# Four batches per step in two buffers, in place of two batches in four, in the last loop of a graph-attention and slot-expert kernel

## The chip, the cores and the metric

The kernel runs on one core of a Trainium2 chip. The metric is the device time of one execution in microseconds; the median of three runs of the kernel before is 3202.54 us (3198.05 to 3209.62).

## The reference

Input `x` is 64 batches of 128 tokens with 384 features. The reference adds a graph-attention layer to it, and then a mixture-of-slots layer with 8 x 4 experts:

```
x = x + L0_gnn_ref(layernorm(x), adj, ...)      # attention with bias adj, then a feed-forward layer
x = x + L0_ffn_ref(layernorm(x), ...)           # slots, 32 experts, then:
#   out2 = einsum('bGkpd,bGksp->bGksd', o, comb2)      expert rows back to slots
#   out  = einsum('bGPd,bGgP->bGgd', out2, comb1)      slots back to tokens
```

The last two products are merged in the kernel: the dispatch stage has already multiplied the two combine matrices into one 128 x 128 matrix per batch, `combT`. What is left for the last stage is, for each of the 64 batches, one product of that matrix with the 128 x 384 rows of expert output, plus the 128 x 384 rows of the residual.

## The kernel before, in words

There are four stages, each in its own block, one after the other: the attention layer, `dispatch`, `experts` and `combine`. Only `combine` (from L1707) is touched.

`combine` walks over the 64 batches in 8 rounds of `ROUND` = 8 batches. A round is cut into steps of `G` batches, one per buffer, so that there are `BUF = ROUND // G` buffers; with `G` = 2 there are four buffers of two batches. Each buffer is three tiles: `o_sb[i]` ("c_o", expert rows), `ct[i]` ("c_ct", combine matrices) and `y[i]` ("c_y", the result), and `G` PSUM banks. Whatever `G` is, there are 8 batches' worth of each.

- SP's queue: `body` waits until the matmuls that read the buffer a round ago are done (`full`, L1743), then issues one load of expert rows (L1744) and one of combine matrices (L1745). In the first round it does not wait. After the last step of the first round it also issues one load of the residual of the last 8 batches, `late` ("c_late", L1747). The residual of the first 56 batches (`early`) is in the chip's memory already, in the tile "slots2T".
- TensorE: waits for both loads (`landed[i]`), then does one matmul per batch (L1758), each into its own bank. A float32 matmul of 128 x 128 by 128 x 384 shows in the trace as two matmul instructions, so x4 stands for two batches and x8 for four. A bank must have been read by VectorE a round ago (`added`, L1757).
- VectorE: waits until the store that used `y[i]` a round ago has landed (`stored[i]`), then adds the residual to each bank (L1773).
- ScalarE's queue: waits for the `G` additions of a step and issues one store of `y[i]` to the output (L1780). At the end it waits for all stores.

The order on each queue is that of the code; no scheduler changes it. Round 0 is written out, rounds 1 to 6 are a hardware loop (L1727), and round 7 is written out.

Of the kernel before, what the change touches and what calls it, by code (L numbers as in the profile page):

```python
# [62 lines left out]
def past(step, n):  # L63

    return not isinstance(step, int) or step >= n


def build(nc, x, adj, wq, bq, wk, bk, wv, bv, wo, bo, w1, b1, w2, b2, alpha1, gamma1, alpha2, gamma2,
# [13 lines left out]
    with ExitStack() as kernel_ctx:  # L82
# [28 lines left out]
        with ExitStack() as experts_ctx:  # L111
            slots2T = sb(experts_ctx, "slots2T", [P, E1, DC, NB, S1])

            early = slots2T[:].rearrange("p k c b j -> p (k c b j)")[:, 0:EARLY * D].rearrange("p (g d) -> p g d", d=D)
            res_landed = sem(experts_ctx, "res_landed", 16)
            with ExitStack() as ctx:
                dispatch(nc, ctx, sb, ps, sem, ident, nhalf, eps, f_w_slot2, yn_dram, comb_dram, ct_dram, slots2T)
            with ExitStack() as ctx:
                experts(nc, ctx, sb, ps, sem, ident, slots2T, f_w1, f_b1, f_w2, f_b2, o_dram, res_dram, early,
                        res_landed)  # L120
            with ExitStack() as ctx:
                combine(nc, ctx, sb, ps, sem, ct_dram, o_dram, res_dram, out, early, res_landed)
# [1584 lines left out]
def combine(nc, ctx, sb, ps, sem, ct_dram, o_dram, res_dram, out, early, res_landed):  # L1707


    G = 2  # L1710
    BUF = ROUND // G
    ROUNDS = NB // ROUND
    o_sb = [sb(ctx, f"c_o{i}", [P, G, D]) for i in range(BUF)]
    ct = [sb(ctx, f"c_ct{i}", [P, G, P]) for i in range(BUF)]
    late = sb(ctx, "c_late", [P, NB - EARLY, D])
    y = [sb(ctx, f"c_y{i}", [P, G, D]) for i in range(BUF)]
    bank = [[ps(ctx, f"c_bank{i}{g}", [P, 512]) for g in range(G)] for i in range(BUF)]
    landed = [sem(ctx, f"c_landed{i}", 32) for i in range(BUF)]
    stored = [sem(ctx, f"c_stored{i}", 16) for i in range(BUF)]
    full, added = sem(ctx, "c_full", ROUND), sem(ctx, "c_added", ROUND)  # L1720
    out_rows = out.rearrange("b n d -> (b n) d")

    def loop(eng, body):

        for i in range(BUF):
            body(0, i)
        with eng.Fori(1, EARLY // ROUND) as r:  # L1727
            for i in range(BUF):
                body(r, i)
        for r in range(EARLY // ROUND, ROUNDS):  # L1730
            for i in range(BUF):
                body(r, i)

    def rows_of(t, r, i):

        return t[bass.ds(r * (ROUND * P) + i * G * P, G * P), :].rearrange("(g p) d -> p g d", p=P)

    with nc.Block() as block:
        @block.sync
        def _(sp):  # L1740
            def body(r, i):
                if past(r, 1):
                    sp.wait_ge(full.sem, full.at(r - 1, G * (i + 1)))  # L1743
                sp.dma_start(o_sb[i][:], rows_of(o_dram, r, i)).then_inc(landed[i].sem, 16)  # L1744
                sp.dma_start(ct[i][:], ct_dram[bass.ds(r * ROUND + i * G, G)].rearrange("g p n -> p g n")).then_inc(landed[i].sem, 16)  # L1745
                if isinstance(r, int) and r == 0 and i == BUF - 1:
                    sp.dma_start(late[:], res_dram[EARLY * P:NB * P, :].rearrange("(g p) d -> p g d", p=P)  # L1747
                                 ).then_inc(res_landed.sem, 16)
            loop(sp, body)

        @block.tensor
        def _(pe):
            def body(r, i):
                pe.wait_ge(landed[i].sem, landed[i].at(r, 32))
                for g in range(G):
                    if past(r, 1):
                        pe.wait_ge(added.sem, added.at(r - 1, G * i + g + 1))  # L1757
                    pe.matmul(bank[i][g][:, 0:D], ct[i][:, g, :], o_sb[i][:, g, :], start=True, stop=True).then_inc(full.sem, 1)  # L1758
            loop(pe, body)

        @block.vector
        def _(dve):
            def body(r, i):
                if past(r, 1):
                    dve.wait_ge(stored[i].sem, stored[i].at(r - 1, 16))
                for g in range(G):
                    if isinstance(r, int) and r * ROUND >= EARLY:
                        dve.wait_ge(res_landed.sem, 16 * (EARLY // ROUND + 1))
                        x_of = late[:, r * ROUND + i * G + g - EARLY, :]
                    else:  # L1770
                        x_of = early[:, bass.ds(r * ROUND + i * G + g, 1), :].rearrange("p o d -> p (o d)")
                    dve.wait_ge(full.sem, full.at(r, G * i + g + 1))  # L1772
                    nc.vector.tensor_tensor(y[i][:, g, :], bank[i][g][:, 0:D], x_of, ALU.add).then_inc(added.sem, 1)  # L1773
            loop(dve, body)

        @block.scalar
        def _(act):
            def body(r, i):
                act.wait_ge(added.sem, added.at(r, G * (i + 1)))
                act.dma_start(rows_of(out_rows, r, i), y[i][:]).then_inc(stored[i].sem, 16)  # L1780
            loop(act, body)
            for s in stored:
                act.wait_ge(s.sem, 16 * ROUNDS)
# [24 lines left out]
```

## Time and profile before

| | us |
|---|---|
| median of three runs | 3202.54 |
| the three runs | 3209.62, 3198.05, 3202.54 |
| profiled execution, its own time | 3206.89 |
| span of the profiled execution | 3205.1 |
| last matmul of `experts` ends | about 3113.7 of the span |
| first load of `combine` issued | 3118.07 of the span |

The profiled execution's own time is 1.8 us over its span. The last stage is the stretch from 3118 us to the end of the span, 87 us. Times below are microseconds from the start of the span. The DMA share of a stretch is the mean busy share of the 16 DMA engines; since packets overlap within an engine it reads a little over 1 when they are full. The granted clock of TensorE is 1.00 at 2.4 GHz and 0.50 at 1.2 GHz.

### The profile page before, as it was taken

What the parts mean: (1) busy time and instruction counts of PE and PEld (TensorE: products, weight loads), DVE (VectorE), ACT (ScalarE), POOL (GpSimd) and SP (SyncE); (2) the same over time, 40 slices, a digit from 0 to 9 for tenths busy, and PEclk for the clock granted to TensorE, in tenths of its full rate; (3) what the DMA queues carried; (4) which work ended last, traced back from release to release, by engine and by line L of the source; (5) the groups of instructions that cost most, each with busy time, mean ns of one, the idle gap of its engine ahead of it and who ended that gap; (6) DMA issues with size and microseconds to landing.
All of it is one profiled execution on the core that took longest, in us unless ns stands there. A gap on an engine that the chain in (4) does not pass through costs nothing. (4 is left out here: it accounts for less than half of the span.)

```text
span 3205.1 us, 63021 instructions
## 1 busy us (share of the span) xinstructions
PE 2945.6 (92%) x21523; PEld 2821.3 (88%) x21523; DVE 1867.8 (58%) x2989; ACT 1541.1 (48%) x3982; POOL 1474.4 (46%) x1486
## 2 busy tenths in 40 slices
PE   3999999999999999999999858888799999999986
PEld 3899999999999999999999847777799999999982
DVE  4456556565655656565655525545476777777754
ACT  3354554545454554545454435455445554545430
POOL 0334444343434444343444434343276777676750
PEclk9999999999999999999999979899899999999999
DMA  4000101010100101010110123433466666666869
GB/s 125 29 24 29 39 25 44 25 44 23 42 27 25 44 25 44 25 44 23 35 34 25 34 82 107 123 104 93 147 212 203 213 199 209 205 217 206 264 224 365
DMA packets 289909, 320.75 MB, mean 100 GB/s; under 512 B 23688, under 2 KB 289416, under 8 KB 289800
## 3 DMA queue, kind: packets, MB, share of 16 engines
q1 hardware_dynamic: 281128, 307.17, 30.6%
q10 hardware_dynamic: 8704, 12.58, 1.1%
q8 instruction: 45, 0.74, 0.1%
q14 instruction: 32, 0.26, 0.0%
HBM read 260.97 MB, written 58.72 MB: 100 GB/s over the span
## 5 line engine op out<-in xcount | busy, mean ns | idle before, releaser
L1537 PE MATMUL u_bank<-x_in,x_w 128*128 128x256 f32 x4608 | 574.1, 283 | 5.6 <-DVE x_w L1625 5.6
L1537 PEld LDWEIGHTS u_bank<-x_in,x_w 128*128 128x128 f32 x4608 | 569.2, 192 | 5.8 <-issue 5.8
L927 POOL TENSOR_TENSOR hT_lo<-h_tmp,hT_hi 128x512 fp32r<-128x512 f32 x192 | 247.9, 1291 | 473.3 <-DVE hT_hi L815 473.3
L1694 POOL TENSOR_TENSOR x_aT<-x_act,x_aT 128x512 fp32r<-128x512 f32 x128 | 299.5, 2340 | 181.9 <-ACT x_aT L1602 181.9
L388 PE MATMUL m_bank<-yT_hi,w_hi 128*128 128x256 f32 x1152 | 339.6, 295 | 0.0
L388 PE MATMUL m_bank<-yT_lo,w_hi 128*128 128x256 f32 x1152 | 324.5, 282 | 0.0
L388 PE MATMUL m_bank<-yT_hi,w_lo 128*128 128x256 f32 x1152 | 323.7, 281 | 0.0
L1690 POOL TENSOR_TENSOR x_w<-raw,x_w 128x768 fp32r<-128x768 f32 x128 | 274.2, 2142 | 105.1 <-DVE x_w L1633 105.1
L661 ACT ACTIVATE h_tmp<-m_bank,b1c 128x256 f32<-128x256 f32 x384 | 160.8, 470 | 329.8 <-PE m_bank L388 329.4
L1593 ACT ACTIVATE x_gelu<-u_bank,x_b1T 128x256 f32<-128x256 f32 x256 | 121.9, 476 | 409.6 <-PE u_bank L1537 409.6
L1549 PE MATMUL o_bank<-x_w,x_aT 128*128 128x384 f32 x1536 | 287.8, 335 | 1.8 <-POOL x_aT L1694 1.8
L1625 DVE TENSOR_TENSOR x_w<-raw,x_w 128x1536 fp32r<-128x1536 f32 x128 | 225.6, 1763 | 99.5 <-ACT x_w L1576 99.5
L388 PE MATMUL f_bank<-w_hi,hT_hi 128*128 128x384 f32 x768 | 279.7, 364 | 1.0 <-POOL hT_lo L927 1.0
L1549 PEld LDWEIGHTS o_bank<-x_w,x_aT 128*128 128x128 f32 x1536 | 262.1, 188 | 2.2 <-issue 2.2
L388 PE MATMUL f_bank<-w_lo,hT_hi 128*128 128x384 f32 x768 | 259.9, 338 | 0.0
L388 PE MATMUL f_bank<-w_hi,hT_lo 128*128 128x384 f32 x768 | 259.6, 338 | 0.0
L628 ACT ACTIVATE s_sb<-s_sb,nmax 128x128 f32<-128x128 f32 x512 | 198.0, 389 | 63.2 <-DVE nmax L775 63.2
L815 DVE CAST hT_hi<-h_tmp 128x512 fp32r<-128x512 f32 x192 | 81.7, 426 | 240.9 <-ACT h_tmp L661 240.9
L388 PEld LDWEIGHTS m_bank<-yT_lo,w_hi 128*128 128x128 f32 x1152 | 217.5, 189 | 4.1
L388 PEld LDWEIGHTS m_bank<-yT_hi,w_hi 128*128 128x128 f32 x1152 | 216.2, 188 | 4.1
L388 PEld LDWEIGHTS m_bank<-yT_hi,w_lo 128*128 128x128 f32 x1152 | 217.3, 189 | 0.0
L1651 DVE SCALAR_TENSOR_TENSOR x_act<-u_bank,x_b1T,x_gelu 128x256 f32<-128x256 f32 x256 | 119.8, 478 | 138.3 <-ACT x_gelu L1593 138.3
(213 smaller groups left out, 7303.8 us busy)
## 6 DMA issues: line engine op xcount, KB each, us to landing
raw<-in_L_ffn_w_dram SPq DMA_DIRECT2D x384, 384.0 KB, 4.8
ws_raw<-in_L_ffn_w_slot_dram SPq DMA_DIRECT2D x32, 576.0 KB, 4.2
x_in<-in_x_dram SPq DMA_DIRECT2D x32, 384.0 KB, 3.4
x_res<-in_x_dram SPq DMA_DIRECT2D x32, 384.0 KB, 4.1
residual<-f_sb SPq DMA_DIRECT2D x32, 384.0 KB, 2.5
yn<-yn_sb SPq DMA_DIRECT2D x32, 384.0 KB, 2.5
d_yn<-yn SPq DMA_DIRECT2D x64, 192.0 KB
expert_out<-x_o SPq DMA_DIRECT2D x64, 192.0 KB, 3.1
```

The source lines that it names most:

```text
L388: mm = pe.matmul(dst, left, right, start=start and c == 0 and j == 0, stop=stop and c == n - 1 and j == 2)
L628: nc.scalar.activation(s, s, ACT.Exp, bias=nmax[:, t, h:h + 1], accum_out=ssum[:, t, h:h + 1]).then_inc(p_ok.sem, 1)
L661: nc.scalar.activation(h_tmp[i % 2][:, half, :], m_bank[i % 2][:, half, :], ACT.Silu, bias=b1c[:, 2 * i + half:2 * i + half + 1]).then_inc ...
L815: nc.vector.tensor_copy(hT[i % 3][0][:], h_tmp[i % 2][:]).then_inc(hh.sem, 1)
L927: nc.gpsimd.tensor_tensor(hT[i % 3][1][:], h_tmp[i % 2][:], hT[i % 3][0][:].bitcast(F32), ALU.subtract).then_inc(hl.sem, 1)
L1537: mm = pe.matmul(u_bank[n % BANKS][:, g, :], w1s[i % 2][a][:, c, g, c2 * P:(c2 + 1) * P], xT[e % 2][b][:, c, :], start=c == 0 and j == 0, ...
L1549: mm = pe.matmul(o_bank[e % 2][t][:, 0:D], aTs[i % 2][a][:, c2, t * P:(t + 1) * P], w2s[i % 2][b][:, c2, :], start=i == 0 and c2 == 0 and ...
L1593: nc.scalar.activation(gel[:, c2, :], u_bank[n % BANKS][:, 1, :], ACT.Gelu_apprx_tanh, bias=b1T[:, HID // P + n, bass.ds(x, 1)]).then_inc( ...
L1625: nc.vector.tensor_tensor(w1s[i % 2][1][:], raw1[i][:], w1s[i % 2][0][:].bitcast(F32), ALU.subtract).then_inc(w1_lo.sem, 1)
L1651: nc.vector.scalar_tensor_tensor(out=aT[i % 2][:, c2, :], in0=u_bank[n % BANKS][:, 0, :], scalar=b1T[:, n, bass.ds(x, 1)], in1=gel[:, c2, ...
L1690: nc.gpsimd.tensor_tensor(w2s[i % 2][1][:], raw2[i][:], w2s[i % 2][0][:].bitcast(F32), ALU.subtract).then_inc(w2_lo.sem, 1)
L1694: nc.gpsimd.tensor_tensor(aTs[i % 2][1][:], aT[i % 2][:], aTs[i % 2][0][:].bitcast(F32), ALU.subtract).then_inc(al.sem, 1)
```

## The change

`G` goes from 2 to 4, and with it `BUF` from 4 to 2. Every tile keeps its total size: two buffers of four batches in place of four of two. Each load and each store is twice as large, and there are half as many. The contiguous piece that a packet moves stays as it was (one row of 384 or of 128 floats). A buffer is refilled after four matmuls in place of two, and a store is issued after four additions in place of two.

```
 def combine(nc, ctx, sb, ps, sem, ct_dram, o_dram, res_dram, out, early, res_landed):
 
 
-    G = 2
+    G = 4
     BUF = ROUND // G
     ROUNDS = NB // ROUND
     o_sb = [sb(ctx, f"c_o{i}", [P, G, D]) for i in range(BUF)]
```

The instructions of TensorE, VectorE and GpSimd keep their kinds and their order. On SP's queue the start of the last stage reads so before, where a tile's number is that of its buffer:

```order
L1744 DMA c_o0<-expert_out 128x2x384
L1745 DMA c_ct0<-combT 128x2x128
L1744 DMA c_o1<-expert_out 128x2x384
L1745 DMA c_ct1<-combT 128x2x128
L1744 DMA c_o2<-expert_out 128x2x384
L1745 DMA c_ct2<-combT 128x2x128
L1744 DMA c_o3<-expert_out 128x2x384
L1745 DMA c_ct3<-combT 128x2x128
L1747 DMA c_late<-residual 128x8x384
```

and so in the changed kernel:

```order
L1744 DMA c_o0<-expert_out 128x4x384
L1745 DMA c_ct0<-combT 128x4x128
L1744 DMA c_o1<-expert_out 128x4x384
L1745 DMA c_ct1<-combT 128x4x128
L1747 DMA c_late<-residual 128x8x384
```

Four loads stand ahead of the residual load where there were eight. On ScalarE's queue the stores of the loop's body and of the last round change so (the register and wait instructions between them go too):

```order
-L1780 DMA out_dram<-c_y 128x2x384
+L1780 DMA out_dram<-c_y 128x4x384
 L1727 REGISTER_ALU
 L1727 COMPARE_AND_BRANCH
-L1780 DMA out_dram<-c_y 128x2x384 x4
+L1780 DMA out_dram<-c_y 128x4x384 x2
 L1738 UNCONDITIONAL_BRANCH
```

The last round has two stores in place of four, and the very last one carries four batches.

## Rows read from the trace of the kernel before

**Rows 1.** Chain of waits, window 3100 to 3206: shares of the chain by engine and line.

```profile
by line: DMA c_ct<-combT 40.6%; PE c_bank L1758 23.2%; SPq L1744 4.7%; DVE c_y L1773 3.7%; issue 3.3%; SPq L1745 3.3%; DVEq L1773 0.3%; SPq L1727 0.1%; SPq L1743 0.1%; DVEq L1772 0.1%
```

**Rows 2.** Busy time, granted clock, DMA share and GB/s by stretch.

```profile
core 0: us, PE busy (x) PEld busy (x) DVE busy (x) ACT busy (x) POOL busy (x), PEclk, DMA share, GB/s
3118.00:3205.10 87.10, 53.32 (x128) 24.69 (x128) 35.59 (x64) 0.00 (x0) 0.00 (x0) 0.90 1.01 356
3155.00:3190.00 35.00, 23.14 (x60) 10.16 (x60) 16.98 (x31) 0.00 (x0) 0.00 (x0) 1.00 1.08 388
3119.00:3130.00 11.00, 6.69 (x13) 3.81 (x14) 2.83 (x6) 0.00 (x0) 0.00 (x0) 0.58 0.98 316
...
3135.00:3138.00 3.00, 2.20 (x4) 1.17 (x4) 0.41 (x1) 0.00 (x0) 0.00 (x0) 0.53 1.07 392
3140.00:3144.00 4.00, 4.00 (x10) 2.23 (x10) 2.23 (x4) 0.00 (x0) 0.00 (x0) 0.75 0.90 275
3146.00:3150.00 4.00, 1.72 (x5) 0.85 (x6) 1.98 (x4) 0.00 (x0) 0.00 (x0) 1.00 1.06 378
3200.00:3202.00 2.00, 1.42 (x4) 0.54 (x4) 1.03 (x2) 0.00 (x0) 0.00 (x0) 1.00 0.71 258
3202.00:3203.00 1.00, 0.00 (x0) 0.00 (x0) 0.08 (x1) 0.00 (x0) 0.00 (x0) 1.00 0.00 0
```

**Rows 3.** DMA issues of the last stage: count, KB each, median us to landing.

```profile
c_o<-expert_out SPq DMA_DIRECT2D x32, 384.0 KB, 6.4
out_dram<-c_y ACTq DMA_DIRECT2D x32, 384.0 KB, 6.1
c_ct<-combT SPq DMA_DIRECT2D x32, 128.0 KB, 7.0
c_late<-residual SPq DMA_DIRECT2D x1, 1536.0 KB, 9.7
```

**Rows 4.** Tile c_ct: the second load's landing; then of all loads issued 3160 to 3190.

```profile
DMA to landing us min/median/max: 5.2/5.2/5.2
...
DMA to landing us min/median/max: 6.3/7.0/7.9
```

**Rows 5.** Tile c_y: the first store's landing (issued 3126.86), then the last store's.

```profile
DMA to landing us min/median/max: 6.8/6.8/6.8
...
DMA to landing us min/median/max: 2.5/2.5/2.5
```

**Rows 6.** Timeline, first two rounds: start, us, instruction, idle before and releaser.

```profile
3119.51 0.47 SPq L1745 DMA_DIRECT2D c_ct<-combT  x1
...
3123.01 0.47 SPq L1747 DMA_DIRECT2D c_late<-residual  x1
...
3123.31 7.90 PE L1758 MATMUL c_bank<-c_o,c_ct 128*128 128x384 f32 x16 [9.61 <-DMA c_ct<-combT]
...
3126.41 0.39 SPq L1744 DMA_DIRECT2D c_o<-expert_out  x1
...
3135.80 2.92 PE L1758 MATMUL c_bank<-c_o,c_ct 128*128 128x384 f32 x4 [4.59 <-DMA c_ct<-combT]
...
3149.83 1.55 PE L1758 MATMUL c_bank<-c_o,c_ct 128*128 128x384 f32 x4 [1.71 <-DMA c_ct<-combT]
```

**Rows 7.** Chain of waits: four batches on TensorE at the low and at full clock.

```profile
3123.31 5.33 PE c_bank L1758 x8
...
3158.17 2.97 PE c_bank L1758 x8
```

**Rows 8.** Timeline, steady part: first and last of 13 TensorE steps, a refill.

```profile
3161.92 1.55 PE L1758 MATMUL c_bank<-c_o,c_ct 128*128 128x384 f32 x4 [0.80 <-DVE c_y L1773]
...
3163.65 0.37 SPq L1744 DMA_DIRECT2D c_o<-expert_out  x1
...
3190.16 1.55 PE L1758 MATMUL c_bank<-c_o,c_ct 128*128 128x384 f32 x4 [0.81 <-DVE c_y L1773]
```

**Rows 9.** Timeline, the last step.

```profile
3199.86 0.94 PEld L1758 LDWEIGHTS c_bank<-c_o,c_ct 128*128 128x128 f32 x4 [1.52 <-DMA c_ct<-combT]
...
3200.91 1.17 DVE L1773 TENSOR_TENSOR c_y<-c_bank,c_late 128x384 f32<-128x384 f32 x2 [1.29 <-PE c_bank L1758]
...
3202.12 0.38 ACTq L1780 DMA_DIRECT2D out_dram<-c_y  x1
```

More of the change, by code:

```diff
@@ L1707, in combine @@
 def combine(nc, ctx, sb, ps, sem, ct_dram, o_dram, res_dram, out, early, res_landed):
-    G = 2
+    G = 4
     BUF = ROUND // G
```

## Prediction

> **What bounds the kernel now.** Only the last stage changes, so I read that stage alone: first the chain of waits from 3100 on, then busy time by stretch, then the DMA issues with their time to landing, then the timeline of the first rounds, a steady piece and the end. What the reader is to see: the chain spends 40.6% of its time in loads of combine matrices and 23.2% in matmuls [rows 1], which looks like a stage bound by the round trip of its buffers. The stretches say otherwise. From 3155 to 3190 the DMA engines have a share of 1.08 and move 388 GB/s [rows 2]; TensorE is busy 23 of these 35 us and VectorE 17, so neither is the limit. One step of two batches moves 0.393 MB of expert rows, 0.131 MB of matrices and 0.393 MB of output [rows 3], 0.917 MB, which is 2.36 us at 388 GB/s; the steps themselves start at 3161.92 and, 12 steps later, at 3190.16 [rows 8], which is 2.35 us each. So the steady part runs at the rate of the DMA engines, and the chain only shows which transfer happened to be waited for.
>
> The whole stage moves 32 x 0.917 MB and the residual's 1.57 MB, 30.9 MB, or 79.7 us at 388 GB/s, and lasts 87.1 us [rows 2]. The 7.4 us between are: 1.0 us before the first byte (3118 to 3119); the first 11 us at 316 GB/s, which cost 11 x (1 - 316/388) = 2.0 us; a slump at 3140 to 3144, 4 x (1 - 275/388) = 1.2 us; and the end: 2 us at 258 GB/s (0.7 us), 1.0 us with no byte moved, and about 1.1 us of the last 2.1 us [rows 2]. That sums to 7.0 us. The bytes, the packets (same rows, same sizes) and the matmuls don't change. So the question is only what becomes of these 7 us, and whether two buffers still keep the DMA engines full.
>
> **The steady part with two buffers.** What the trace shows of a transfer with nothing ahead of it is the last store: issued at 3202.12, no byte moved before 3203.0, landed after 2.5 us [rows 2, 5, 9]. Its 0.393 MB take 1.0 us at 388 GB/s, so a transfer costs 1.5 us beside its bytes, 0.9 ahead of them and 0.6 behind. A new load of four batches is 1.05 MB, 2.7 us; a new store 0.79 MB, 2.0 us; a step of four batches is 4.73 us at full rate, and each buffer has 2 x 4.73 = 9.46 us for its round.
>
> Round of a load buffer, with nothing ahead of it in the DMA engines: from the last of four matmuls 0.15 us to the issue (the step that starts at 3161.92 is over at 3163.5, and the refill is issued at 3163.65 [rows 8]), 0.9, 2.7, 0.6, about 0.1 to TensorE's start, and 2.97 us for four batches at full clock [rows 7]: 7.4 us. That leaves 2.1 us of the 9.46 for queueing behind stores. If instead a store shares the engines half and half with the load as soon as it comes (1.8 us after the matmuls: 0.7 for the last addition, 0.2 to the issue, 0.9), the load has 0.75 us alone and its other 1.95 us take 3.9: the round is 9.3 us, with 0.16 us to spare. The round of an output tile: four additions 2.4 us (two take 1.17 [rows 9]), 0.2 to the issue, 1.5 and 2.0, in all 6.1 us, which leaves 3.4 us for a load of 2.7 ahead of it. So both rounds fit at either end, the one by 2.1 us and the other by next to nothing.
>
> Which end is nearer? Loads land 6.4 to 7.0 us after their issue and stores 6.1 [rows 3], so both see the same queue. And the first store, issued at 3126.86, took 6.8 us [rows 5]. At 3127.8 it came behind what was left of the first 3.67 MB (2.10 MB of loads and the residual) and behind a refill: some 0.8 to 0.9 MB and 0.5 MB, 3.5 us or more, with its own 1.0 and the 1.5 a little over 6 us. Half of the engines from the start would have landed it after 1.5 + 2 x 1.0 = 3.5 us. So a transfer waits for what was issued before it, and I take the end with 2.1 us to spare.
>
> The Trainium skill, "DMA: Bandwidth & Descriptors", section "Queues, rings and completion order", says the opposite: that each DMA engine takes turns between the queues it has work for, packet by packet. By that the loads would share with the stores as in the second sum above, and two buffers would be at the edge. The first store does not bear it out.
>
> What remains is scatter. In the steady part the loads' landings range from 6.3 to 7.9 us about 7.0 [rows 4]. With four buffers the other three hide that. With two, 0.9 us late at every other step would be 0.4 us per step, 5 us over the 13 steps between start and end; with 2.1 us to spare it is nearly nothing. Bounds 0 and +5; I take +1.3 us.
>
> **The start.** The first buffer is ready when four batches have landed, in place of two: the second pair's matrices were issued at 3119.51 and landed 5.2 us later, at 3124.7 [rows 4, 6], against 3123.31 for the first matmul now [rows 6]. The clock is at 0.50 then, and four batches take 5.33 us as they do now [rows 7]: they end at 3130.1, the refill is issued at 3130.25 and has its first byte at 3131.15; now the first refill goes out at 3126.41 [rows 6]. What covers the gap is the first 3.67 MB; now 3.48 MB have moved by 3130.0 (11 us x 316 GB/s [rows 2]), so it lasts to 3130.5. The DMA engines stand idle 0.65 us: +0.7 us, and up to +1.1 if the first loads go out faster, which gives the same back. Four issues ahead of the residual where there are eight could do that; bounds -0.5 and 0, I take 0.
>
> **The slump.** Now the first refill is behind the residual, TensorE waits 4.59 us [rows 6], its clock is at 0.50 when it starts again (0.53 from 3135 to 3138 [rows 2]), and refills come late, so the DMA engines run dry at 3140 to 3144. With the change the second buffer is computed from 3130.1 to 3133.1 at full clock, the first refill lands by 3134.5, and TensorE waits 1.4 us, less than the 1.71 us [rows 6] after which the clock is still at 1.00 [rows 2]. The slump goes: -1.2 us; at the other end it stays, 0.
>
> **The end.** Order of the last transfers: the last load, then the stores of steps 13, 14 and 15 (of 0 to 15). The last load's bytes are in 4.05 us before store 14's end; then 0.6, 0.1, 2.97 us of matmuls, 0.7 for the last addition, 0.1 and 0.9 give 5.4 us: 1.3 us without a byte. The additions of step 15 must also wait until the store of step 13 has landed in the same `y` tile, 2.6 us after the last load's bytes; four additions, 0.1 and 0.9 from there make 6.0 us: 2.0 us idle. Now it is 1.0 idle and 0.7 of lower rate [rows 2]. Change: -0.4 to +0.3, I take +0.3.
>
> **Fewer instructions.** SP and ScalarE issue 48 transfers fewer. Their issues lie beside full DMA engines: nothing.
>
> The Trainium skill's same page, section "Bandwidth", asks for transfers of 1 MiB or more to get 75% of peak. By that, twice the size would raise the rate. The trace has 388 GB/s with 384 KB and 128 KB transfers, since several are in flight.
>
> **The sum.** +1.3 + 0.7 - 1.2 + 0.3 = +1.1 us on a profiled 3206.89: 3208.0. That execution is 4.35 us above the median of the runs, 3202.54, so on the median 3203.6 us, a change of 0.03%. About 0.3%, 9.6 us, is what a measurement of this kernel can tell from no change; the three runs alone span 11.6 us.
>
> **Rivals.**
> - *The buffers' round is exposed and TensorE falls to 1.2 GHz: slower.* If load and store share the engines half and half (round 9.3 us) and TensorE's waits of near 2 us are enough for the low clock, four batches take 5.33 in place of 2.97 us: the round is 11.7 us, a step 5.8 in place of 4.73, and 14 steps cost +15 us: 3218. It decides in each gap between two bursts of TensorE: the clock must fall. For it: the low clock was there after a wait of 4.59 us [rows 2, 6]. Against: at 1.71 us it stayed, and transfers queue in order [rows 5].
> - *Exposed at full clock.* The scatter costs its upper bound, 5 us, and the slump stays: +7 us, 3210.
> - *Larger transfers fill the engines better: faster.* At most the 7 us of lower rate can be won, of which the first byte's 1.0 and about 2 at the end cannot: -4 us, 3199. For it: the slump goes and the start has half the issues. Against: the packets are the same, and the DMA share is 1.08 already.
> - *The change does not do what it says.* The order of SP's queue shows that it does.
>
> **Chances.** Forecast (within 3 us) 0.62; exposed at full clock 0.17; larger transfers better 0.10; low clock 0.08; anything else 0.03. Only the low clock is beyond 0.3%, and part of the exposed case with the scatter of the runs; on the fast side only the scatter is. Slower 0.12, same 0.84, faster 0.04. The range is 3196 to 3214: the forecast, 3199 and 3210 with the scatter of a median of a few runs, some 4 us. It leaves the low clock out.
>
> **What would show it.** The steady part's steps of four batches take 4.7 us at 388 GB/s, with TensorE waiting 1.4 to 2 us at clock 1.00. No wait above 3 us and no stretch at half clock after 3131. A short gap in the DMA engines near 3130.5, no slump near 3142. First matmul at 3124.7. The last store's issue to landing 3.5 us, with about 2 us idle ahead of it. I am wrong if the DMA rate in the steady part is below 380 GB/s, or if the low clock comes back after the start.

## The result, and the profile after

The changed kernel takes 3230.13 us (median of 5 runs, 3221.01 to 3235.57), the kernel before 3205.28 us beside it (5 runs): a ratio of 1.0075, interval 1.0055 to 1.0094, 24.9 us slower. Timed again on another chip it is 1.0061 (1.0037 to 1.0084). The prediction was 3203.6 us, no change, with a range of 3196 to 3214. It was wrong.

The profiled execution has a span of 3233.8 us, and its last stage starts with the first load at 3124.16, 6.1 us later than before, although nothing ahead of it was changed. Over all the profiles of this study that start lies between 3108.8 and 3124.4 us, so this part is scatter of the untouched stages. The stage itself, first load to end of span, is the number to compare: 87.0 us before, 109.6 us after (104.4 us in a second profile).

Busy time by stretch for the changed kernel, with the columns of [rows 2]:

```profile
3124.20:3233.80 109.60, 63.47 (x128) 31.32 (x128) 34.75 (x64) 0.00 (x0) 0.00 (x0) 0.76 0.85 283
3161.20:3196.20 35.00, 23.60 (x49) 11.34 (x49) 13.45 (x26) 0.00 (x0) 0.00 (x0) 0.79 0.94 304
```

The second row lies as far into the stage as the steady row of before, which had 388 GB/s and clock 1.00 [rows 2]. Now it has 304 GB/s and 0.79: the DMA engines are no longer full, and TensorE no longer at full clock. The same bytes are moved at 283 GB/s over the stage. The chain of waits (window 3100 to 3234) is still led by loads and matmuls, and the matmuls' share has grown from 23.2% [rows 1]:

```profile
by line: DMA c_ct<-combT 42.7%; PE c_bank L1758 27.9%; SPq L1744 2.5%; issue 1.6%; DVE c_y L1773 0.4%; SPq L1745 0.3%; DVEq L1772 0.0%
```

The issues, to be read against [rows 3]: half as many, twice the size, and the medians to landing have hardly changed for the loads.

```profile
c_o<-expert_out SPq DMA_DIRECT2D x16, 768.0 KB, 5.8
out_dram<-c_y ACTq DMA_DIRECT2D x16, 768.0 KB, 7.6
c_ct<-combT SPq DMA_DIRECT2D x16, 256.0 KB, 7.5
c_late<-residual SPq DMA_DIRECT2D x1, 1536.0 KB, 12.4
```

Two rounds of the two buffers in the timeline (start, us, instruction, idle before and releaser):

```profile
3175.74 5.48 PE L1758 MATMUL c_bank<-c_o,c_ct 128*128 128x384 f32 x8 [3.18 <-DMA c_ct<-combT]
...
3181.40 0.37 SPq L1744 DMA_DIRECT2D c_o<-expert_out  x1
...
3182.42 2.84 PE L1758 MATMUL c_bank<-c_o,c_ct 128*128 128x384 f32 x8 [1.19 <-DMA c_ct<-combT]
...
3185.43 0.38 SPq L1744 DMA_DIRECT2D c_o<-expert_out  x1
...
3187.65 4.54 PE L1758 MATMUL c_bank<-c_o,c_ct 128*128 128x384 f32 x8 [2.39 <-DMA c_ct<-combT]
...
3194.18 4.25 PE L1758 MATMUL c_bank<-c_o,c_ct 128*128 128x384 f32 x8 [2.00 <-DMA c_ct<-combT]
```

The refill issued at 3181.40 reaches TensorE at 3187.65, 6.25 us later; the one issued at 3185.43 at 3194.18, 8.75 us later. Each refill waits for a burst of four batches, and a burst takes 2.84 us at full clock, 4.25 to 5.48 when a part of it or all of it runs at the low one. So a buffer's round is near 12 us where two steps at the DMA engines' rate are 9.46, and in the round there are stretches in which the only load on its way has just been issued and moves few bytes. This is the stretch after the issue at 3181.40. TensorE starts on the other buffer's load at 3182.42, and the store issued at 3182.22 moves no packet before 3186.5 (shown further below):

```profile
3181.00:3182.00 1.00, 0.23 (x1) 0.00 (x0) 0.50 (x1) 0.00 (x0) 0.00 (x0) 0.59 0.55 166
3182.00:3184.00 2.00, 1.58 (x5) 1.06 (x6) 0.58 (x2) 0.00 (x0) 0.00 (x0) 1.00 0.50 68
3184.00:3185.00 1.00, 1.00 (x4) 0.38 (x2) 0.83 (x3) 0.00 (x0) 0.00 (x0) 1.00 0.81 287
3185.00:3187.00 2.00, 0.26 (x1) 0.00 (x0) 0.87 (x2) 0.00 (x0) 0.00 (x0) 1.00 1.05 357
```

Until 2.6 us after the issue the engines move little, and they are full only some 3 us after it.

### The profile page after: what moved, and what is told of

It is laid out like the page before. It is cut to its first block and busy times, and to the rows that moved or that the text cites. A ratio compares the mean times of both kernels' runs of the same rounds, so it can differ in the third digit from the quotient of the medians.

```text
span 3233.8 us, 62874 instructions
## 1 busy us (share of the span) xinstructions
PE 2961.8 (92%) x21523; PEld 2833.9 (88%) x21523; DVE 1867.6 (58%) x2989; ACT 1540.1 (48%) x3982; POOL 1473.6 (46%) x1486
```

## The experiments

Two numbers are used for each kernel: the ratio and the stage. The ratio to the kernel before, with its interval, is of 4 to 10 runs. The stage is read from one profile, first load of the last stage to the end of the span. Three more are worked out from the timeline of that profile, over the last seven of the eight rounds: the median time from a refill's issue to TensorE's start on it; the mean length of a burst on TensorE over one buffer (all rounds); and the period of a buffer's step.

| kernel | ratio (interval) | stage | issue to TensorE | burst | period |
|---|---|---|---|---|---|
| before, two batches | 1 | 87.0 | 7.7 | 1.7 | 2.37 |
| changed, four batches | 1.0075 (1.0055, 1.0094) | 109.6 | 7.9 | 4.0 | 5.95 |
| e5 changed, again | 1.0061 (1.0037, 1.0084) | 104.4 | 8.7 | 3.7 | 5.88 |
| e1 changed, loop written out | 1.0039 (1.0023, 1.0055) | 103.3 | 8.2 | 3.8 | 5.86 |
| e6 before, loop written out | 1.0005 (0.9989, 1.0021) | 87.6 | | | |
| e7 loads of 4, stores of 2 | 1.0046 (1.0030, 1.0062) | 104.8 | 9.0 | 3.9 | |
| e8 loads of 2, stores of 4 | 1.0000 (0.9985, 1.0016) | 87.0 | 7.8 | 1.6 | 2.37 |
| e3 four load buffers | 0.9996 (0.9982, 1.0010) | 89.5 | 14.2 | 3.4 | |
| e11 three load buffers | 0.9996 (0.9979, 1.0013) | 91.0 | 11.2 | 3.5 | 4.75 |
| e4 four store buffers | 1.0036 (1.0016, 1.0055) | 101.4 | | | |
| e2 clock kept up | 1.0049 (1.0034, 1.0065) | 102.8 | 8.8 | 3.2 | 5.89 |
| e10 short matmuls | 1.0022 (1.0004, 1.0039) | 93.0 | 9.1 | 1.65 | 5.07 |
| e9 large matrix packets | 1.0047 (1.0031, 1.0062) | 107.0 | 8.3 | 3.9 | |
| e13 refill in two transfers | 1.0076 (1.0052, 1.0100) | 109.4 | 8.6 | 4.0 | 6.30 |
| e14 and landing by halves | 0.9995 (0.9978, 1.0012) | 91.0 | 6.9 | 1.8 | 2.55 |
| e15 few stores | 0.9994 (0.9980, 1.0008) | 85.4 | 5.4 | 3.5 | 4.64 |
| e12 two batches, eight buffers | 0.9997 (0.9983, 1.0011) | 86.9 | | | |

For all but e2 and e5 the last stage's loop is written out, so that loads and stores can have sizes and buffer counts of their own:

```
-    G = 4
-    BUF = ROUND // G
+    GL, NL = 4, 2          # batches per load, load buffers
+    GS, NY = 4, 2          # batches per store, store buffers
...
+            for j in range(NB // GL):
+                i = j % NL
+                if j >= NL:
+                    sp.wait_ge(full.sem, GL * (j - NL + 1))
```

**Is it the loads or the stores?** The controls first.

> The changed last stage with its hardware loop written out, nothing else: two load buffers and two store buffers of four batches. It is the control for the runs beside it. Every theory expects what the changed kernel did: from the first load's issue to the end of the span 109.6 us (3124.2 to 3233.8), against 87.0 before, ratio to the kernel before near 1.0075. If it were the loop's branches that cost, it would be under 100 us.

> The changed kernel once more, as the control on this chip. Ratio 1.005 to 1.009, stage 103 to 110 us.

> The last stage with its loop written out, but two batches per step in four buffers as in the kernel before. Control for the writing out: ratio within 0.2% of 1, stage 86 to 89 us.

Written out, the kernel before is as it was (1.0005, 87.6 us). The changed one is somewhat less slow written out (1.0039 against 1.0061 and 1.0075), with intervals that touch; a stage of 103.3 us, below what I had written for e1, lies beside the 104.4 of e5. Whether the hardware loop has a small part of its own is not settled. The runs below are compared with e1.

e7 has `GL, NL = 4, 2` and `GS, NY = 2, 4`; e8 has it the other way round.

> Loop written out. Loads of four batches in two buffers as in the changed kernel, stores of two batches in four tiles as in the kernel before. Load-round theory: the loss is in the loads alone, stage 98 to 105 us, ratio 1.003 to 1.006. Store theory: under 92 us.

> Loop written out. Loads of two batches in four buffers as in the kernel before, stores of four batches in two tiles as in the changed kernel. Load-round theory: stage 86 to 91 us, ratio within 0.2% of 1. Store theory: 98 us or more.

Both came out as the load-round theory had it. Stores of four batches in two tiles cost nothing at all; VectorE even waits 40.3 us for them in e8, and the DMA engines stay full:

```profile
DVE c_y L1759 <- DMA out_dram<-c_y: 40.3, 14, 5.2
3147.90:3182.90 35.00, 23.36 (x60) 10.16 (x60) 14.14 (x30) 0.00 (x0) 0.00 (x0) 1.00 1.08 387
```

(the first row is of the waits: who waited for whom, us in total, times, longest; the second is busy time by stretch). Loads of four in two buffers cost all that e1 loses (1.0046 beside 1.0039).

**Buffers.** e3 is `NL = 4`, e11 `NL = 3`, e4 `NY = 4`, each with everything else as in e1.

> Loop written out, transfers of four batches as in the changed kernel, but four load buffers (16 batches) in place of two; stores keep two. Round-trip theory: DMA engines never run empty on loads, the stage is 86 to 90 us. Low-clock theory without a buffer shortage: 100 or more. Store theory (VectorE waits for the store of the same tile, which lands 7.6 us after issue): hardly better than 109.6, since additions and banks still wait. Size theory (a large transfer itself is slower): over 100.

> Written-out loop, transfers of four batches, three load buffers (12 batches) in place of two. The load's round may then last three steps, 14.2 us. Load-round theory: it is 11 to 12 us, so three are enough, stage 88 to 91 us, ratio within 0.2% of 1. If four batches in flight at a time need more than that: 95 us or more.

> Loop written out, transfers of four batches, two load buffers as in the changed kernel, but four store buffers (16 batches). Store theory: the stage falls under 95 us. Round-trip and low-clock theories: 105 to 110 us, as the loads' round is unchanged.

A third load buffer is enough, with transfers of four batches throughout. e3's and e11's steady stretches:

```profile
3161.10:3196.10 35.00, 23.83 (x61) 12.38 (x60) 13.62 (x28) 0.00 (x0) 0.00 (x0) 0.89 1.08 387
```

```profile
3148.60:3183.60 35.00, 24.29 (x60) 12.87 (x61) 13.66 (x28) 0.00 (x0) 0.00 (x0) 0.89 1.08 385
```

387 and 385 GB/s, although the clock is at 0.89 and some bursts still take 4.5 us: with a buffer to spare a slow burst does not lower the rate. The stages of 89.5 and 91.0 us are still 2.5 to 4 us longer than before, too little for the ratios to show. More store tiles alone leave a stage of 101.4 us, under the 105 to 110 I had written but beside e1's 103.3. VectorE's waits for stores, 15.9 us in e1, were a sign and not the cause.

**TensorE's clock and its time.** e2 adds this to the changed kernel. Ahead of the filler stands one more wait, for the addition that reads the bank that the filler writes into (left out here):

```
+                for n in range(FILL_FIRST if first else FILL):   # 14, 7
+                    pe.matmul(bank[i][0][:, D:D + P], ident[:], ident[:], start=True, stop=True)
                 pe.wait_ge(landed[i].sem, landed[i].at(r, 32))
```

> The changed kernel, with matmuls of the identity by itself that nobody reads (14 before the first step, 7 before each later one, about 1.5 us at full clock) ahead of TensorE's wait for the loads, so that its clock stays up. Low-clock theory (TensorE's bursts of four batches take 4.3 to 5.5 us at half clock in place of 2.85, which delays the refills): the stage falls from 109.6 us to 92 or less. Round-trip theory (a refill is issued only after four batches, and the DMA engines run empty between): the low clock is a third to a half of it, the stage is 97 to 103 us. If the clock is a mere sign, 108 or more.

The stage is 102.8 us, in the round-trip theory's range but close to what the changed kernel itself shows in its second profile (104.4). The filler raised the clock from 0.76 to 0.92 over the stage and shortened the mean burst from 4.0 to 3.2 us, but not every burst: after a wait of 2.45 us behind the filler one still took 4.54 us. It also puts 1.7 us of its own ahead of any load that lands early, and the step stays at 5.89 us. The ratio, 1.0049 (1.0034 to 1.0065), lies below the changed kernel's 1.0075 and 1.0061, but its interval overlaps both of theirs. So a gain from the higher clock is not shown by this run, and the clock's part in the loss stays open.

e10 reads both operands as fp32r (`.bitcast(F32R)`), so that a batch is one matmul instruction.

> Written-out loop, two load buffers of four batches, with one-pass matmuls on the same data read as fp32r (less exact products), so that four batches take near 1 us on TensorE in place of 2.9 to 5.5. If the matmuls between a landing and the next issue are a full part of the load's round, 2 to 4 us shorter rounds of two steps fit into 9.5 us again and the stage falls from 104 us to 88 to 93. If TensorE's time is hidden and only the transfers count: 100 us or more.

93.0 us, the edge of the first theory's range. Bursts are 1.65 us though the clock is at 0.50 all through, and 10 of e1's 103.3 us go: TensorE's time between a landing and the next issue is a part of the round. It is no cure, 1.0022: the issue-to-start time grows to 9.1 us, the step is 5.07 us, and the steady part is still short of 388 GB/s. That the two loads now come closer together and share the engines more would explain the growth, but was not tried.

```profile
3158.40:3193.40 35.00, 11.53 (x28) 7.97 (x28) 12.87 (x28) 0.00 (x0) 0.00 (x0) 0.50 1.04 352
```

**What makes the refill slow?** e9 reads the matrices of a buffer as one piece per partition:

```
-                sp.dma_start(ct[i][:], ct_dram[j * GL:(j + 1) * GL].rearrange("g p n -> p g n"))
+                sp.dma_start(ct[i][:].rearrange("p g n -> p (g n)"), ct_dram[j * GL:(j + 1) * GL].rearrange(
+                    "g (a c) n -> (g a) (c n)", c=GL))
```

> Written-out loop, two load buffers of four batches, but the combine matrices are read as one contiguous piece of 2048 bytes per partition in place of four of 512 (the same number of bytes, in another order, so the products are of other numbers than the reference's). Packet theory: while load and store take turns packet by packet, a 512-byte packet beside a 1536-byte one leaves the matrices about 90 GB/s, so 0.26 MB take up to 3 us; with large packets the load's round loses 1 to 2.5 us and the stage falls from 104 us to 93 to 99. If the lead-in of a load and the four matmuls are what counts: 101 to 105 us.

The packet theory fell: 107.0 us, no better than e1 and above both ranges, and the issue-to-start time stays at 8.3 us. The small packets are not what sets the round.

e13 issues each refill as two pairs of transfers of the old size, one behind the other; e14 gives each half its own semaphore, and TensorE waits for it alone:

```
+                for h in range(0, GL, 2):
+                    b = j * GL + h
+                    sp.dma_start(o_sb[i][:, h:h + 2, :], rows_of(o_dram, b, 2)).then_inc(landed[...].sem, 16)
+                    sp.dma_start(ct[i][:, h:h + 2, :], ct_dram[b:b + 2].rearrange("g p n -> p g n")).then_inc(landed[...].sem, 16)
```

> Written-out loop, two load buffers of four batches, refilled after four matmuls and waited for as a whole, as in the changed kernel, but each refill is two pairs of transfers of the old size. If only the coarse refill and landing count: stage 101 to 108 us, as with the large transfers. If the large transfer itself is slow: under 95 us.

> As the run before, and TensorE waits for each half of a buffer by itself, so that two batches can be computed while the other half is under way. The load's round loses the bytes and matmuls of a half, 1.4 us or more of some 12, and more at the low clock: stage 92 to 100 us. If the refill alone (after four matmuls) set the loss: 101 us or more. If landing alone did: under 90 us.

e13, with transfers as small as before but two coarse buffers, is as slow as the changed kernel (109.4 us, 1.0076, a little over the 101 to 108 I had written), and its steady part is as empty:

```profile
3148.60:3183.60 35.00, 20.47 (x43) 10.76 (x42) 11.71 (x21) 0.00 (x0) 0.00 (x0) 0.79 0.85 284
```

So no part of the loss can be put down to the size of a transfer; it goes with what is waited for. e14, at 91.0 us and 0.9995, lies between what I had written for refill and landing together (92 to 100) and for the landing alone (under 90): with the refill as coarse as in the changed kernel, letting TensorE start on the first half takes the loss away as far as the ratio shows. The stage is still 4 us longer than before, and four batches take 2 x 2.55 = 5.1 us where the engines' rate would allow 4.73. The burst that stands between a landing and the refill falls from four batches to the last two, the other half's bytes lie under the first two matmuls, and the clock stays at 1.00 in the steady part:

```profile
3151.20:3186.20 35.00, 22.43 (x59) 9.87 (x58) 16.08 (x30) 0.00 (x0) 0.00 (x0) 1.00 1.07 375
```

e15 issues one store of four and leaves the other rows of the output unwritten:

> Written-out loop, two load buffers of four batches, three of four stores left out (their rows of the output are not written). If sharing with stores stretched the refills: the median from a refill's issue to TensorE's start falls from 8.2 us to 6.2 to 6.8, and the stage to 80 to 90 us, although 9.4 MB less are moved, which at the full rate would be 24 us. If the lead-in and the matmuls are nearly all: median 7.5 us or more, stage over 92 us.

The median from issue to TensorE's start falls from 8.2 to 5.4 us, below what I had written, and the least is 5.3. The timeline of one refill, in which all packets that the engines move up to 3159.2 are of the loads' queue:

```profile
3153.77 0.37 SPq L1733 DMA_DIRECT2D c_o<-expert_out  x1
...
3159.14 4.30 PE L1747 MATMUL c_bank<-c_o,c_ct 128*128 128x384 f32 x8 [2.82 <-DMA c_ct<-combT]
```

5.4 us is thus a refill of 1.05 MB with no store's bytes beside it, and the 2.5 us up to the changed kernel's 7.9 come with the stores. Part of these may be the other buffer's load, which lies beside it longer when the round is longer. Nor is all of it shared bandwidth: the changed kernel's refill of 3181.40 took 6.25 us although no store moved a packet before 3186.5. Even alone the round of 0.15 + 5.4 + 3.5 us leaves only 0.4 us of the 9.46.

**A better version?**

> A version that might beat both: two batches per step, eight load buffers and eight store tiles, loop written out. The steady part is at the rate of the DMA engines already, so only the starved stretches near the start (1 to 2 us) can be won: stage 85 to 87 us against 87.0, ratio within 0.2% of 1. If the depth of the queue still cost something in the steady part: under 84 us.

86.9 us and 0.9997: no gain to be measured. The steady part is at 389 GB/s, and none of the kernels run here beats the kernel before.

## Why the prediction was wrong, step by step

**What bounds the kernel now** was right: the steady part of before is at the DMA engines' rate, and what would decide is whether two buffers keep them full. Both of the signs named for being wrong came: 304 GB/s in the steady part, below 380, and the low clock after the start.

**The steady part** is the step that failed. "So both rounds fit at either end" is false for the load buffer. The sum had three mis-sized terms:

- The refill by itself, issue to TensorE's start: 0.9 + 2.7 + 0.6 + 0.1 = 4.3 us; e15 measured 5.4. I took the lead-in from a store. A load starts more slowly: after 3181.40 the engines are full only 3 us later, and after e15's issue at 3153.77 about 2 us later. The trace of before had this in it: its very first load was issued at 3118.07 and TensorE started at 3123.31 [rows 6], 5.2 us for half the bytes with no store anywhere, though with other loads issued right behind it.
- Sharing with stores. I worked out the half-and-half end and set it aside, on the ground that the first store took 6.8 us [rows 5]. The DMA queues of the changed kernel show the sharing as it is, first from 3159 to 3162 and then from 3192 to 3193, where the loads move rows of the matrices (q1 carries the loads, q10 the stores; packets, MB, time of the packets as a share of 16 engines):

```profile
q1 hardware_dynamic: 395, 0.60, 53.4%
q10 hardware_dynamic: 394, 0.58, 51.7%
...
q10 hardware_dynamic: 189, 0.29, 76.8%
q1 hardware_dynamic: 188, 0.10, 31.7%
```

  395 packets of the one against 394 of the other, and then 188 against 189, though the loads' packets are a third of the size: the turns go by packets and not by bytes. The rule in the Trainium skill, "DMA: Bandwidth & Descriptors", section "Queues, rings and completion order", by which each engine takes turns between its queues packet by packet, holds here, and I had rejected it. The trace of before has it too, in its steady part, from 3178 to 3179:

```profile
q10 hardware_dynamic: 159, 0.24, 64.6%
q1 hardware_dynamic: 158, 0.15, 42.1%
```

  The first store of before was late for another reason: from 3127.8 to 3130.8 the engines of the kernel before moved packets of the loads' queue only, although the store had been issued at 3126.86,

```profile
q1 hardware_dynamic: 668, 1.01, 101.7%
```

  so its packets came late to the engines, 4 us after the issue. Full engines are not needed for such a delay. In the changed kernel the store of 3182.22, issued behind a refill of 3181.40, moves no packet up to 3186.5 either, while the engines have room (68 GB/s from 3182 to 3184). This is all that they moved from 3182.2 to 3186.5:

```profile
q1 hardware_dynamic: 844, 0.95, 77.7%
```

  The last store of before, with no load issued ahead of it, started after 0.9 us [rows 2, 9]. So the delay goes with a load issued just ahead; by what means is not shown. The stores cost up to 2.5 us a refill (7.9 against 5.4).
- The burst: 2.97 us at full clock; measured 4.0 on the mean, as the clock fell.

Together 0.15 + 7.9 + 4.0 = 12.1 us, 6.03 per step; the period measured is 5.95 against 4.73. Thirteen steps at 1.2 us are 16 us of the 22.6 us by which the stage of this profile grew. Two slips in the same part change nothing: the terms of the half-and-half round add up to 9.37 us and not 9.3, and 0.45 us of scatter over 13 steps is 5.9 us and not 5.

**The slower rival** was the mechanism that happened: half-and-half sharing, TensorE at the low clock, 5.8 us a step, 3218 us. It had a chance of 0.08. Its step is right within 3%, but by luck: it has 6.2 us from the issue to TensorE's start (9.3 less 0.15 and 2.97) where 7.9 were measured, and bursts of 5.33 us where the mean was 4.0, and the two errors cancel. It also missed the start and the end. And its point of decision was put wrongly, for the low clock alone does not make the loss: e15's period is 4.64 with six of its 16 bursts slowed by the low clock, and e11 has five such bursts and no measurable loss. Nor does the loss need it in most bursts: in e2 the mean burst is 3.2 us and the step still 5.89 us, the filler's own time included. The point from which it decides is whether the round fits into the buffers' time. With the measured 7.9 us it does not even at full clock (0.15 + 7.9 + 2.97 = 11.0 against 9.46); that TensorE's waits then bring the low clock, whose longer bursts lengthen the round further, fits the trace but was not taken apart.

**The start** was to cost 0.7 us and the slump near 3142 to go. The first matmul came 7.4 us after the first issue, against 6.6 predicted (3124.7 less 3118.07), and two slumps came in place of one, the first as large as 5 us at 127 GB/s:

```profile
3135.00:3140.00 5.00, 4.87 (x12) 2.38 (x10) 2.93 (x7) 0.00 (x0) 0.00 (x0) 0.76 0.46 127
3140.00:3145.00 5.00, 0.00 (x0) 0.00 (x0) 0.46 (x1) 0.00 (x0) 0.00 (x0) 0.93 1.05 365
...
3150.00:3155.00 5.00, 4.03 (x11) 1.99 (x9) 3.25 (x6) 0.00 (x0) 0.00 (x0) 0.89 0.37 100
```

  The reason is in the main the same lead-in: I had the engines idle for 0.65 us between the first 3.67 MB and the refill. The refill was issued 13.0 us after the first load (3137.19 less 3124.16) where I had 12.2, and the engines were full only at 3140.0, 2.8 us after that.

**The end** was to change by -0.4 to +0.3 us. The last load's landing was followed by a burst at the low clock, and the engines moved almost nothing from 3225 to 3230, with the last store's first byte after 3230.5:

```profile
3223.56 5.49 PE L1758 MATMUL c_bank<-c_o,c_ct 128*128 128x384 f32 x8 [3.97 <-DMA c_ct<-combT]
```

```profile
3225.00:3230.00 5.00, 4.05 (x7) 1.69 (x5) 2.23 (x4) 0.00 (x0) 0.00 (x0) 0.54 0.01 4
```

  From TensorE's start to the end of the span it is 10.2 us, against 5.2 before (3199.86 [rows 9] to 3205.1).

**Scatter and issues.** That 48 issues fewer bring nothing was right, as e13 and e8 show from both sides. The size rule of the same page of the Trainium skill, section "Bandwidth", brings nothing here either: e13 has the old sizes and the new loss, e11 the new sizes and no loss.

## What to carry to other kernels

Before the number of buffers is halved, add up the whole round of a buffer: refill alone, as a load of that size shows it and not a store, its share with the traffic beside it, and all the work between the landing that is waited for and the issue of the next refill. If it comes near the number of buffers times the step, the step will follow the round, however well the DMA engines were filled before. Larger transfers don't need coarser waits: waiting by halves (e14) or one more buffer (e11) keeps the step at or near the engines' rate (5.1 and 4.75 us against 4.73), and a coarse store, which nobody waits for at once, is free (e8).

## What the runs showed of the hardware

- A load that finds the DMA engines empty moves few bytes at first: 68 GB/s from 3182 to 3184 and 287 in the next microsecond, for an issue at 3181.40. The refill of e15 issued at 3153.77 was quicker, with 114 GB/s in its second microsecond and 358 in its third. The last store of before had nothing ahead of it either, and its 0.39 MB landed 2.5 us after the issue [rows 5].
- A store issued just behind a load of four batches moved its first packet only after 4.3 us (3182.22, and no packet up to 3186.5), one issued with no load ahead after 0.9 us (3202.12 in the kernel before).
- TensorE's granted clock can fall inside a burst. The burst of 3187.65 ran at full clock for its first microsecond and at the low one for the rest, the one of 3175.74 at the low clock throughout:

```profile
3187.65:3188.60 0.95, 0.95 (x3) 0.67 (x4) 0.00 (x0) 0.00 (x0) 0.00 (x0) 1.00 1.06 401
3188.70:3192.00 3.30, 3.30 (x6) 1.35 (x4) 1.58 (x3) 0.00 (x0) 0.00 (x0) 0.50 1.06 396
...
3175.74:3181.20 5.46, 5.46 (x8) 2.52 (x8) 1.67 (x3) 0.00 (x0) 0.00 (x0) 0.50 1.07 395
```

- The clock fell after shorter waits than I had allowed for, but the length of the last wait does not settle it. A burst of four batches takes 2.84 us at full clock. In the changed kernel bursts after waits of 1.19, 1.74 and 1.89 us took 2.84 to 2.85 us; after 2.00, 2.23 and 2.39 us they took 4.25, 4.48 and 4.54 us; and after 3.96 and 3.97 us 4.47 and 5.49 us. In other runs bursts after longer waits stayed at full clock: 2.85 us after a wait of 2.42 us in e1, after 3.30 us in e9, and here in e4:

```profile
3167.46 2.85 PE L1747 MATMUL c_bank<-c_o,c_ct 128*128 128x384 f32 x8 [3.20 <-DMA c_ct<-combT]
```
